# Slopes of the recurrent layer: one store per chunk from the history, in place of four stores in each step

## The chip, the cores and the metric

The program runs on one core of a Trainium2 chip, in one launch. The metric is device time in microseconds, the median of three runs. Engines are named as in the profile: PE (matmul), PEld (its weight load), DVE, ACT, POOL, and SP, whose only work here is to issue DMAs and to wait for them. SPq in a row is SP's queue of instructions.

## What is computed

A tower of five layers on 64 sequences of 248 tokens with 64 features: a convolution over tokens, attention, a sparse feed-forward layer, a recurrent layer whose weights are learned while it reads, and a mixture of experts. The change is in the fourth. Cut to what matters:

```python
def step(carry, xs):
    cp, cm = carry                       # weights W0 [64,256], W1 [256,64] and P0, P1; their momenta
    k_t, v_t, q_t, a_t, th_t, e_t = xs
    g = jax.vmap(jax.grad(loss_fn))(cp, k_t, v_t)         # mean((mlp(k) - v)^2)
    nm = m * e_t - th_t * g              # for each of the four
    np_ = p * (1 - a_t) + nm
    return (np_, nm), _mlp(np_, q_t)     # silu(h @ (W0+P0)) @ (W1+P1)
_, ys = jax.lax.scan(step, (cur_p, cur_m), xs)            # 248 steps, one after the other
```

## The kernel before

The recurrent layer (`recurrent_layer`) takes 249 steps in 16 chunks (`NCH`), `CH` = 16 steps in each of the first 15 and 9 in the last. Within a chunk the weights are not updated step by step. Each step's hidden row `h`, output row `y` and slope `dl` (the gradient at the hidden layer, 256 wide, two copies of 64 sequences) go to a history on chip, `hist`, whose partition is 16 times a group of sequences plus the step, and later steps read the past from there. At the head of the next chunk, the update, the 16 steps are folded into the weights.

The first layer's weights are handled differently: a step needs only the product of keys and weights, so the update works it out for the 16 coming steps ("base") from all earlier slopes. These lie in memory, in `DXD` (the profile calls it between_slopes), one row of 64 x 256 numbers for each step. The update reads them back in pieces of 512 KB into a ring of three tiles that share space with `hdiag` (`load_slopes`, L2091), 16 pieces in chunks 0 to 8 and 32 in chunks 9 to 15. A table of products of keys, `CT`, comes in beside them (`load_table`, L2085).

SP works its instructions off in the order in which they are written:

- at a chunk's head: wait until the other engines have begun the chunk; four or six loads of the table; wait for `hist_d`, the semaphore on which all of the last chunk's slopes count; three loads of slopes; then eight loads `cc` (L2137) and eight `alt` (L2142); then, as PE finishes each of 16 groups ("bg"), more loads of slopes and tables and the stores of the base (L2156);
- in each step: load the base of the next step (L2063), eight copies of `h` to the history (`to_hist`, L2074), load a value (L2066), eight copies of `y` and one store of it (L2176), eight copies of `dl` to the history, and four stores of `dl` to `DXD` (L2180). The copies and the stores of `dl` count on one semaphore, `hist_d`: 8 + 4 DMAs in each step.

The lines that wait for slopes on PE: in a step, before the first matmul that reads the history of slopes (L2330), for the twelve DMAs of the step before; in the update, before the matmuls of each group X (L2287), for the pieces in the ring. The update on PE is a chain over X = 0 to 15: `new_terms` (L2254), `turned` (L2267), `from_slopes` (L2280 with the table's first part, L2287 with the slopes). PE goes on to the next X only when it is through with `from_slopes` of this one.

Of the kernel before, what the change touches and what calls it, by code (L numbers as in the profile page):

```python
# [11 lines left out]
B, L, D, DIN, HID = 64, 248, 64, 128, 256  # L12
TL = L // 2
FS = 8
NH = 8
CH, NCH = 16, 16
# [24 lines left out]
class Space:  # L41
# [8 lines left out]
    def sem(self, name):  # L50
        return self.ctx.enter_context(self.nc.semaphore(f"{self.name}_{name}"))
# [48 lines left out]
def settled(e, sem):  # L100


    e.nop().then_inc(sem, 1)
# [884 lines left out]
def key_layer(nc, W_fused, H2, ZR, VR, GR, DXD, CT):  # L988
# [3 lines left out]
    with ExitStack() as ctx:  # L992
# [3 lines left out]
        zero = S.sb("zero", [128, 64 * D])  # L996
# [6 lines left out]
        s_own, s_own_sp, s_own_pe = S.sem("settled"), S.sem("settled_sp"), S.sem("settled_pe")  # L1003
        s_id, s_w, s_z, s_v, s_t = S.sem("ident"), S.sem("weights"), S.sem("zeros"), S.sem("set_v"), S.sem("set_t")
# [7 lines left out]
        out = Loop(S.sem("out"), ["z"], 16 * 8, 0)  # L1012
        with nc.Block() as block:
# [10 lines left out]
            @block.sync  # L1024
            def _(e):
                e.dma_start(wr[:, 0, :], W_fused[0:128, :]).then_inc(s_w, 16)
                e.dma_start(wr[0:NF - 128, 1, :], W_fused[128:NF, :]).then_inc(s_w, 16)

                e.wait_ge(s_v, 1)
                z3 = lambda k: zero[:, 0:k * D].rearrange("p (t d) -> p t d", d=D)  # L1030
                nz = 0
                for t0 in range(0, VR.shape[0], 64):
                    k = min(64, VR.shape[0] - t0)
                    e.dma_start(VR[t0:t0 + k, :, :].rearrange("t p d -> p t d"), z3(k)).then_inc(s_z, 16)
                    nz += 1
                e.dma_start(ZR[0:CH + 1, :, :].rearrange("t p d -> p t d"), z3(CH + 1)).then_inc(s_z, 16)
                k = ZR.shape[0] - CH - L
                e.dma_start(ZR[CH + L:, :, :].rearrange("t p d -> p t d"), z3(k)).then_inc(s_z, 16)
                e.dma_start(GR[L:, :, :].rearrange("t b g -> t (b g)"), zero[0:CH * NCH - L, 0:4 * B]).then_inc(s_z, 16)
                nz += 3  # L1040
                for t0 in range(0, CH * NCH, 32):
                    e.dma_start(DXD[t0:t0 + 32, :, :].rearrange("t b f -> (t b f)").rearrange("(p f) -> p f", p=128), zero[:, :]).then_inc(s_z, 16)
                    nz += 1
                for c0, c1, r0, r1 in ((0, 4, 128, 192), (9, 12, 256, 320)):
                    for c in range(c0, c1):
                        e.dma_start(CT[c, r0:r1, :, :], zero[0:64, 0:2048].rearrange("p (g f) -> p g f", g=16)).then_inc(s_z, 16)
                        nz += 1

                e.wait_ge(s_z, 16 * nz)
                with e.Fori(0, 4) as j:  # L1050
                    with e.Fori(0, 4) as q:
                        n = 4 * j + q
                        VE.wait(e, n, "kn")
                        settled(e, s_own_sp)
                        AE.wait(e, n, "v")
                        settled(e, s_own_sp)
                        for a in range(2):
                            t0 = TL * a
                            for w, (dst, row) in enumerate(((ZR[CH + 1 + t0:CH + 1 + t0 + TL], 16), (ZR[CH + t0:CH + t0 + TL], 0), (VR[t0:t0 + TL], 0))):
                                e.dma_start(dst[:, bass.ds(32 * j + 4 * q + row, 4), :], kqv[:, w, a:8:2, :]).then_inc(out.sem, 16)  # L1060
                            e.dma_start(GR[t0:t0 + TL, bass.ds(4 * n, 4), :], gt[:, a:8:2, :]).then_inc(out.sem, 16)
                out.count(e, B // 4)
# [546 lines left out]
RT = 64 + CH * NCH  # L1609
# [222 lines left out]
def recurrent_layer(nc, CT, DXD, VR, GR, YR, BASED, W0, P0, W1, P1):  # L1832
# [8 lines left out]
    with ExitStack() as ctx:  # L1841
# [3 lines left out]
        def sem(name):  # L1845
            return ctx.enter_context(nc.semaphore(name))

        HD, D = 256, 64
# [5 lines left out]
        hist = sb("hist", [128, 8, 2 * HD + D])  # L1854
# [18 lines left out]
        dl = sb("dl", [128, HD])  # L1873
# [17 lines left out]
        DX = 3  # L1891

        ring = [hdiag[:, :, :, :, :].rearrange("p a r j f -> p (a r j f)")[:, 1024 * q:1024 * q + 1024].rearrange("p (j f) -> p j f", j=4) for q in range(DX)]
# [4 lines left out]
        b = [t[:, :] for t in bank]  # L1898
# [45 lines left out]
        base_out = [Stages(sem(f"base_out{q}"), [f"b{k}" for k in range(q, 8, 2)], [], 2 * 16) for q in range(2)]  # L1944
# [4 lines left out]
        value_in = Stages(sem("value_in"), ["first"], ["next"], 16)  # L1949
        hist_h = Stages(sem("hist_h"), [], ["h"], 16 * NH)  # L1950
        hist_y = Stages(sem("hist_y"), [], ["y"], 16 * (NH + 1))
        hist_d = Stages(sem("hist_d"), [], ["d"], 16 * (NH + 4))
        for q in (*sum(dx_in, []), *sum(ct_in, []), *base_out, gates_in, cc_in, al_in, base_in, value_in, hist_h, hist_y, hist_d):
            q.base = 0
        s_set, s_own = sem("set_dma"), sem("settled")
        s_own_pe = sem("settled_pe")
# [119 lines left out]
        def load_gates(e, c):  # L2076
            for q in range(8):
                e.dma_start(gates[16 * q:16 * q + 16, :, :],
                            GR[bass.ds(c * CH, CH), 16 * (q // 2):16 * (q // 2) + 16, :].rearrange("t b g -> b t g")).then_inc(gates_in.sem, 16)

        def load_table(e, c, part, y):

            nb = PARTS[part][2]
            for k, (r0, r1) in enumerate(((0, 64), (64, 192), (192, 320))[:nb + 1]):
                e.dma_start(ct[0:r1 - r0, y % 2, k, :, :].unsqueeze(1), CT[bass.ds(c, 1), r0:r1, 2 * y:2 * y + 2, :].rearrange("a r g f -> r a g f")).then_inc(ct_in[part][y % 2].sem, 16)  # L2085

        def load_slopes(e, part, xk):

            nb = PARTS[part][2]
            g, k = divmod(xk, nb)  # L2090
            e.dma_start(ring[xk % DX], DXD[128 * k:128 * k + 128, g:B:16, :]).then_inc(dx_in[part][xk % DX].sem, 16)  # L2091

        def diag_h(hf):
            return ap(hdiag, hf * 2048, [16, 8], [129, 16])
# [10 lines left out]
        with nc.Block() as block:  # L2105
# [14 lines left out]
            def _(e):  # L2120
                def chunk(c, steps, part):
# [6 lines left out]
                    for yk in range(2):  # L2128
                        load_table(e, c, part, yk)
                    e.wait_ge(hist_d.sem, c * (hist_d.unit * CH))  # L2130
                    settled(e, s_own)
                    for xk in range(DX):
                        load_slopes(e, part, xk)
# [29 lines left out]
                    for s in range(steps):  # L2163
                        e.wait_ge(V.sem, V.step(c, s - 1, "xb") if s else V.upd(c, "x0"))
                        load_base(e, s + 1)

                        e.wait_ge(V.sem, V.step(c, s, "h"))
                        to_hist(e, s, h[:, :], 0, HD, hist_h.sem)
                        if s == 0 and steps == CH:
                            load_gates(e, c + 1)  # L2170
                        e.wait_ge(V.sem, V.step(c, s, "y1"))
                        settled(e, s_own)
                        load_value(e, c, s + 1)
                        e.wait_ge(V.sem, V.step(c, s, "y"))
                        to_hist(e, s, y[:, 0, :], HD, HD + D, hist_y.sem)
                        e.dma_start(YR[bass.ds(c * CH + s, 1), :, :].rearrange("a p d -> p a d"), y[:, 0:1, :]).then_inc(hist_y.sem, 16)  # L2176
                        e.wait_ge(V.sem, V.step(c, s, "d"))
                        to_hist(e, s, dl[:, :], HD + D, 2 * HD + D, hist_d.sem)
                        for j in range(4):
                            e.dma_start(DXD[bass.ds(c * CH + s, 1), 16 * j:16 * j + 16, :].rearrange("a p d -> p a d"),  # L2180
                                        dl[32 * j:32 * j + 16, :].unsqueeze(1)).then_inc(hist_d.sem, 16)

                for part, (first, last, nb) in enumerate(PARTS):
                    with e.Fori(first, min(last, NCH - 1)) as c:
# [356 lines left out]
def audio_tower(nc, x, filt, W_k, b_k, Wqk, Wv, Wpos, bpos, Wproj, bproj, gating, wr, br, w1, b1, w2, b2,  # L2541
                W_fused, W0, W1, P0, P1, Wg, bg, E1, be1, E2, be2, out):

    def scratch(name, *shape):
        return nc.dram_tensor(f"between_{name}", shape, F32, kind="Internal").ap()


    H0, X0, H1, H2, XN = (scratch(n, B, TL, 2, D) for n in ("h_tok", "x_att", "h_att", "h_ffn", "x_ffn"))
    T_ = CH * NCH
    ZR, VR, YR = scratch("keys", T_ + CH + 1, 128, D), scratch("values", T_ + 1, 128, D), scratch("recurrent", T_, 128, D)  # L2550
    GR = scratch("gates", T_, B, 4)
    DXD, CT = scratch("slopes", T_, B, HID), scratch("table", NCH, RT, 16, 128)
    token_layer(nc, x, filt, W_k, b_k, H0, X0)
    attention_layer(nc, Wqk, Wv, Wpos, bpos, Wproj, bproj, gating, H0, X0, H1)
    ffn_layer(nc, wr, br, w1, b1, w2, b2, H1, H2, XN, scratch("w_by_tile", B, L), scratch("w_by_batch", B, L))
    key_layer(nc, W_fused, H2, ZR, VR, GR, DXD, CT)
    table_layer(nc, ZR, GR, CT)
    recurrent_layer(nc, CT, DXD, VR, GR, YR, scratch("base", CH + 1, 128, HID), W0, P0, W1, P1)
    expert_layer(nc, Wg, bg, E1, be1, E2, be2, H2, YR, out)
# [29 lines left out]
```

## Time and profile before

| | |
|---|---|
| median of three runs | 12295.05 us (12288.87 to 12295.21) |
| the profiled execution | 12288.19 us, its span 12286.5 us |
| PE / DVE / ACT busy | 79% / 38% / 16% of the span |
| recurrent layer | from about 3255 us to 11082 us of the span |
| a step | 24.2 us, 249 of them |
| an update | 78 us (chunk 0), 87 to 106 us (chunks 1 to 8), 118 to 135 us (chunks 9 to 15) |
| granted clock of PE | 0.99 in the steps, 0.54 to 0.81 in the updates |

Read it from the outside in: the recurrent layer is nearly two thirds of the span; inside it, steps and updates alternate; each has its own chain of waits.

### The profile page before, as it was taken

How to read it: one execution, taken by the hardware profiler on the slowest of the kernel's cores; microseconds unless marked ns; L12 is line 12 of the kernel's file. 1: busy time of each engine (PE TensorE's matmuls, PEld its weight loads, DVE VectorE, ACT ScalarE, POOL GpSimd, SP SyncE). 2: the span in 40 equal slices, each digit the busy share in tenths (PEclk: the TensorE clock that was granted, in tenths of full speed). 3: DMA queues.
4: the chain of work that ended last, by engine and by line, in shares of the span. 5: the costliest groups of instructions: out<-in, count | busy, mean ns of one | idle time of the engine just before them, and what ended most of it. 6: DMA issues, size and time to landing. Idle time of an engine off the chain costs nothing. (4 is left out here: it accounts for less than half of the span.)

```text
span 12286.5 us, 338221 instructions
## 1 busy us (share of the span) xinstructions
PE 9695.2 (79%) x135922; PEld 5708.6 (46%) x135922; DVE 4669.4 (38%) x11974; ACT 1960.7 (16%) x4398; POOL 232.7 (2%) x167
## 2 busy tenths in 40 slices
PE   5788883523598888888988988889888898896777
PEld 2455551212355555555555555555455555552222
DVE  3444443634723323233233233232332323235555
ACT  1222221211101101011011011110101101012334
POOL 0000000000100000000000000000000000000000
PEclk7999996555898998999999999989898798987888
DMA  2000000143601101011011011120211202020000
GB/s 55 7 7 8 7 8 25 42 123 61 138 17 53 51 18 52 23 47 53 17 53 53 17 53 57 42 81 17 82 45 54 81 17 82 26 72 14 13 10 10
DMA packets 894399, 519.70 MB, mean 42 GB/s; under 512 B 379950, under 2 KB 889462, under 8 KB 892534
## 3 DMA queue, kind: packets, MB, share of 16 engines
q1 hardware_dynamic: 880694, 502.37, 15.1%
q0 software_dynamic: 13312, 12.57, 0.6%
q8 instruction: 188, 3.08, 0.1%
q14 instruction: 205, 1.68, 0.0%
HBM read 323.24 MB, written 154.20 MB: 39 GB/s over the span
## 5 line engine op out<-in xcount | busy, mean ns | idle before, releaser
L2319 PE MATMUL bank<-mv,hdiag 128*32 128x144 f32 x63744 | 2038.0, 289 | 102.1 <-DVE hdiag L2480 102.1
L2319 PEld LDWEIGHTS bank<-mv,hdiag 128*32 128x32 f32 x63744 | 1950.0, 111 | 165.8 <-DVE hdiag L2480 151.2
L2359 PE MATMUL bank<-mvt,ydiag 128*32 128x512 f32 x15936 | 1830.3, 594 | 0.0
L2359 PEld LDWEIGHTS bank<-mvt,ydiag 128*32 128x32 f32 x15936 | 606.5, 109 | 807.8 <-issue 723.1
L2493 DVE TENSOR_TENSOR rep<-bank,wt 128x128 f32<-128x128 f32 x249 | 92.0, 369 | 1863.1 <-PE bank L2319 1863.1
L439 PE MATMUL att_bank<-att_ka,att_qn 128*124 128x496 f32 x1024 | 497.0, 598 | 133.6 <-DVE att_mx L616 67.0
L2423 DVE SCALAR_TENSOR_TENSOR mvt<-mvt,cu,bank 128x256 f32<-128x256 f32 x512 | 223.3, 478 | 791.3 <-PE bank L2254 791.3
L2216 ACT ACTIVATE work<-work 128x128 f32<-128x128 f32 x498 | 142.3, 309 | 2357.6 <-DVE work L2468 2357.6
L2203 ACT ACTIVATE mv<-bank 128x256 f32<-128x256 f32 x1024 | 325.1, 384 | 1091.1 <-PE bank L2267 1091.1
L459 PE MATMUL att_bank<-att_qa,att_ka 128*124 128x248 f32 x2048 | 464.7, 385 | 32.6 <-DVE att_qa L625 32.6
L2254 PE MATMUL bank<-hist,wy 32*128 32x256 f32 x2048 | 393.1, 544 | 90.4 <-DVE wy L2413 89.7
L1555 DVE TENSOR_TENSOR moe_hw<-moe_hb,moe_bank 128x496 f32<-128x496 f32 x512 | 326.4, 669 | 354.5 <-ACT moe_hb L1414 287.0
L2224 ACT ACTIVATE mv<-hdiag 128x128 f32 x249 | 107.8, 433 | 2047.7 <-PE bank L2319 2047.7
L2522 DVE TENSOR_SCALAR work<-bank,wt 128x256 f32<-128x256 f32 x249 | 120.6, 484 | 824.1 <-PE bank L2359 824.1
L2267 PE MATMUL bank<-r_ident,mvt 128*128 128x128 f32 x2048 | 403.9, 362 | 34.6 <-DVE mvt L2431 33.9
L1336 PE MATMUL moe_bank<-moe_x,moe_w 128*128 128x496 bf16 x1536 | 416.8, 415 | 0.0
L459 PEld LDWEIGHTS att_bank<-att_qa,att_ka 128*124 128x124 f32 x2048 | 345.9, 186 | 144.4 <-DVE att_qa L625 48.8
L2287 PE MATMUL bank<-hdiag,ct 128*32 128x256 f32 x2944 | 313.4, 531 | 124.0 <-DMA hdiag<-between_slopes 123.9
L616 DVE TENSOR_REDUCE att_mx<-att_bank 124x2 f32<-124x496 f32 x512 | 339.1, 673 | 166.9 <-PE att_bank L439 163.2
L2267 PEld LDWEIGHTS bank<-r_ident,mvt 128*128 128x128 f32 x2048 | 320.4, 186 | 165.7 <-issue 97.9
L2519 DVE TENSOR_TENSOR ddiag<-bank,mi 128x128 f32<-128x128 f32 x249 | 72.7, 292 | 848.8 <-PE bank L2357 848.8
L2372 PE MATMUL bank<-mvt,r_ident 128*128 128x256 f32 x1494 | 389.0, 396 | 0.0
(402 smaller groups left out, 11450.9 us busy)
## 6 DMA issues: line engine op xcount, KB each, us to landing
hdiag<-between_slopes SPq DMA_DIRECT2D x368, 512.0 KB, 4.6
baset<-between_base SPq DMA_DIRECT2D x265, 128.0 KB, 2.0
between_base<-work SPq DMA_DIRECT2D x256, 128.0 KB
hist<-h SPq DMA_DIRECT2D x1992, 8.0 KB
hist<-y SPq DMA_DIRECT2D x1992, 2.0 KB
hist<-dl SPq DMA_DIRECT2D x1992, 8.0 KB
ct<-between_table SPq DMA_DIRECT2D x184, 128.0 KB, 3.8
between_slopes<-key_zero SPq DMA_DIRECT2D x8, 2048.0 KB
```

What stands on the lines that cost most here:

```text
L439: e.matmul(bank[3 + i % 2][0:TL, 0:2 * L], qn[:, TL * a:TL * a + TL], ka[:, 2 * hp:2 * hp + 2, :], start=True, stop=True).then_inc(T.sem, 1)
L459: mm = e.matmul(bank[3 + h % 2][0:TL, L * mh:L * mh + L], ka[:, h, TL * mh:TL * mh + TL], qa[:, :], start=True, stop=True)
L616: e.tensor_reduce(mx[:, i // 4, 2 * (i % 4):2 * (i % 4) + 2], bank[3 + i % 2][0:TL, 0:2 * L].rearrange("p (h m) -> p h m", h=2), AX, ALU.m ...
L1336: mm = e.matmul(bank[2 + 2 * a + q][:, 0:2 * L], w[:, x_, 128 * a:128 * a + 128], xp[:, 2 * L * q:2 * L * q + 2 * L], start=(k == 0), stop ...
L1555: e.tensor_tensor(hw[:, a, q, :], hb[:, a, q, :], bank[q][:, 0:2 * L], ALU.mult).then_inc(V.sem, 1)
L2203: e.activation(dst, src, ACT.Copy).then_inc(A.sem, 1)
L2254: mm = e.matmul(psNew[X % 2][k][:, HD * w:HD * w + HD], wy[rows, G % 2, w, :, :].rearrange("p u d -> p (u d)"), hist[rows, m * 4 + j, 0:HD ...
L2267: mm = e.transpose(psC[k][:, o:o + 128], mvt[:, 4 * n + j, HD * w + 128 * hf:HD * w + 128 * hf + 128], ident[:, :])
L2287: mm = e.matmul(out[rows, :], ct[:, yk % 2, 1 + k, g % 2, rows], ring[xk % DX][:, j, :], start=False, stop=(k == nb - 1))
L2319: mm = e.matmul(psP[32 * j:32 * j + 32, 0:MW], hdiag[:, hf, r, j, :], mv1[:, hf, r, j, :], start=(hf == 0 and r == 0), stop=(hf == 1 and r ...
L2359: mm = e.matmul(psH[32 * j:32 * j + 32, :], ydiag[:, n, j, :], mvt[:, 4 * n + j, :], start=(n == 0), stop=(n == 7))
L2372: e.matmul(b[1][:, HD:], ident[:, :], mvt[:, k, 0:HD], start=True, stop=True)
```

## The change

The four stores in each step go. At a chunk's head, after the wait for `hist_d`, SP stores the slopes of the last chunk from the history, eight stores of 128 KB (8 groups of 8 sequences, 16 steps each), waits until all eight have landed on a new semaphore `slopes_out`, and loads the first pieces then. `hist_d` counts eight DMAs in each step. `DXD` gets 16 rows in front, so that chunk c can write rows 16c to 16c + 15; chunk 0 writes the zeros with which the history starts. The slopes of the last chunk are not stored, and nobody reads them.

```diff
-        hist_d = Stages(sem("hist_d"), [], ["d"], 16 * (NH + 4))
+        hist_d = Stages(sem("hist_d"), [], ["d"], 16 * NH)
+        slopes_out = Stages(sem("slopes_out"), ["out"], [], 8 * 16)
...
+        SLOPES = DXD[0:CH * NCH, :, :]
...
-            e.dma_start(ring[xk % DX], DXD[128 * k:128 * k + 128, g:B:16, :]).then_inc(dx_in[part][xk % DX].sem, 16)
+            e.dma_start(ring[xk % DX], DXD[CH + 128 * k:CH + 128 * k + 128, g:B:16, :]).then_inc(dx_in[part][xk % DX].sem, 16)
...
                     e.wait_ge(hist_d.sem, c * (hist_d.unit * CH))
+                    settled(e, s_own)
+                    for m in range(2):
+                        for j in range(4):
+                            dst = SLOPES[bass.ds(c * CH, CH), 16 * j + 8 * m:16 * j + 8 * m + 8, :].rearrange("t b f -> b t f")
+                            e.dma_start(dst, hist[:, m * 4 + j, HD + D:]).then_inc(slopes_out.sem, 16)
+                    e.wait_ge(slopes_out.sem, slopes_out.upd(c, "out"))
                     settled(e, s_own)
                     for xk in range(DX):
                         load_slopes(e, part, xk)
...
                         to_hist(e, s, dl[:, :], HD + D, 2 * HD + D, hist_d.sem)
-                        for j in range(4):
-                            e.dma_start(DXD[bass.ds(c * CH + s, 1), 16 * j:16 * j + 16, :].rearrange("a p d -> p a d"),
-                                        dl[32 * j:32 * j + 16, :].unsqueeze(1)).then_inc(hist_d.sem, 16)
...
-    DXD, CT = scratch("slopes", T_, B, HID), scratch("table", NCH, RT, 16, 128)
+    DXD, CT = scratch("slopes", T_ + CH, B, HID), scratch("table", NCH, RT, 16, 128)
```

SP's queue at the head of a chunk before the change, from the last two loads of the table on (ct) to the first of cc; hdiag<-between_slopes are the loads of slopes:

```order
L2085 DMA ct<-between_table 64x256
L2085 ISA
L2085 DMA ct<-between_table 128x256
L2130 REGISTER_ALU
L2091 DMA hdiag<-between_slopes 128x4x256 [waits hist_d]
L2091 DMA hdiag<-between_slopes 128x4x256 x2
L2137 ISA
L2137 DMA cc<-between_table 16x2x128
```

The same place after it; between_slopes<-hist are the new stores, of which the first three and the last stand here:

```order
L2088 DMA ct<-between_table 128x256
L2133 REGISTER_ALU
L2138 ISA [waits hist_d]
L2138 DMA between_slopes<-hist 8x16x256
L2138 ISA
L2138 DMA between_slopes<-hist 8x16x256
...
L2138 ISA
L2138 DMA between_slopes<-hist 8x16x256
L2139 ISA
L2094 DMA hdiag<-between_slopes 128x4x256 [waits slopes_out]
L2094 DMA hdiag<-between_slopes 128x4x256 x2
L2146 ISA
```

Eight stores and a wait for their landing have moved in ahead of the first load of slopes, and with it ahead of all that SP does later in the update.

SP's queue at the end of the first step of a chunk, before the change:

```order
L2074 DMA hist<-y 8x64 x7
L2176 DMA between_recurrent<-y 128x64
L2177 REGISTER_ALU
L2074 DMA hist<-dl 8x256 [waits vector_landed]
L2074 DMA hist<-dl 8x256 x7
L2180 ISA
L2180 DMA between_slopes<-dl 16x256
L2180 ISA
L2180 DMA between_slopes<-dl 16x256
```

And after it:

```order
L2075 DMA hist<-y 8x64 x7
L2185 DMA between_recurrent<-y 128x64
L2186 REGISTER_ALU
L2075 DMA hist<-dl 8x256 [waits vector_landed]
```

Behind the eight copies of `dl` the four stores, each with an instruction ahead that works out its address, are gone, and the next step's load of the base stands there; SP works nothing else off in a different order.

## Rows read from the trace of the kernel before

**Rows 1.** The page: the whole span.

```profile
span 12286.5 us, 338221 instructions
```

**Rows 2.** Waits of SP's queue in the recurrent layer: us in total, times, longest.

```profile
SPq L2074 <- DVE work L2468: 1143.8, 189, 6.5
...
SPq L103 <- DMA between_base<-work: 34.2, 16, 2.2
...
SPq L2189 <- DMA between_slopes<-dl: 1.1, 1, 1.1
```

**Rows 3.** Waits of PE over the whole span, the two for DMAs in the updates.

```profile
PE bank L2287 <- DMA hdiag<-between_slopes: 123.9, 56, 5.1
...
PE bank L2280 <- DMA ct<-between_table: 63.5, 15, 5.0
```

**Rows 4.** Waits of PE in 4820 to 5195 us (15 steps), all of them.

```profile
PE bank L2310 <- DVE h L2475: 16.2, 15, 1.1
PE bank L2323 <- DVE rep L2493: 9.3, 16, 0.6
PE bank L2319 <- DVE hdiag L2480: 6.2, 15, 0.4
PE bank L2345 <- DVE y L2506: 3.3, 16, 0.2
```

**Rows 5.** Timeline of one step: start, length, instructions [idle before].

```profile
5007.94 4.87 SPq L2074 DMA_DIRECT2D hist<-dl  x8
...
5013.01 1.87 SPq L2180 DMA_DIRECT2D between_slopes<-dl  x4
...
5019.32 0.64 PE L2330 MATMUL bank<-hist,adiag 128*32 128x256 f32 x8
5019.43 0.29 DVE L2499 TENSOR_TENSOR gdiag<-bank,mi 128x128 f32<-128x128 f32 x1 [0.39 <-PE bank L2323]
...
5019.89 0.27 PEld L2340 LDWEIGHTS bank<-hist,gdiag 128*32 128x32 f32 x16 [0.42 <-issue]
```

**Rows 6.** Timeline at the head of chunk 3.

```profile
4704.13 4.87 SPq L2074 DMA_DIRECT2D hist<-dl  x8
...
4709.20 1.86 SPq L2180 DMA_DIRECT2D between_slopes<-dl  x4
...
4714.34 3.04 SPq L2085 DMA_DIRECT2D ct<-between_table  x4
4717.59 1.96 SPq L2091 DMA_DIRECT2D hdiag<-between_slopes  x3
4717.82 1.08 PE L2280 MATMUL bank<-w,ct 64*32 64x256 f32 x8 [4.97 <-DMA ct<-between_table]
4719.84 5.93 SPq L2137 DMA_DIRECT2D cc<-between_table  x8
4722.42 1.08 PE L2287 MATMUL bank<-hdiag,ct 128*32 128x256 f32 x8 [3.52 <-DMA hdiag<-between_slopes]
```

**Rows 7.** SP's stores of the base, 128 KB each: issue in ns min/median/max.

```profile
L2156 SPq DMA_DIRECT2D between_base<-work x256: 572/607/701, 3286.2 to 10844.3; - x128
```

**Rows 8.** DMA issues by tile: count, KB each, median us from issue to landing.

```profile
between_table<-tab_ci SPq DMA_DIRECT2D x16, 512.0 KB, 5.6
...
cc<-between_table SPq DMA_DIRECT2D x128, 16.0 KB, 3.0
```

**Rows 9.** Windows: 16 steps, then whole updates (chunks 3, 5, 11, 13); length, busy, PEclk, DMA share, GB/s.

```profile
4812.00:5200.00 388.00, 352.03 (x7158) 226.77 (x7162) 108.44 (x362) 30.74 (x96) 0.00 (x0) 0.99 0.07 17
...
4705.00:4811.00 106.00, 84.58 (x518) 45.17 (x518) 45.70 (x119) 25.43 (x72) 4.19 (x2) 0.60 0.40 120
...
5688.00:5775.00 87.00, 64.31 (x518) 35.29 (x518) 45.34 (x117) 24.58 (x72) 4.19 (x2) 0.76 0.48 147
...
8638.00:8765.00 127.00, 93.98 (x646) 48.60 (x646) 45.23 (x119) 25.33 (x72) 4.19 (x2) 0.64 0.56 175
...
9678.00:9813.00 135.00, 108.41 (x646) 56.45 (x646) 46.04 (x121) 25.76 (x72) 4.19 (x2) 0.54 0.53 165
```

**Rows 10.** Timeline at the head of chunk 0.

```profile
3269.94 1.96 SPq L2091 DMA_DIRECT2D hdiag<-between_slopes  x3
...
3276.88 1.08 PE L2287 MATMUL bank<-hdiag,ct 128*32 128x256 f32 x8
```

**Rows 11.** Timeline at the end of the layer.

```profile
11074.38 4.83 SPq L2074 DMA_DIRECT2D hist<-dl  x8
11079.25 1.82 SPq L2180 DMA_DIRECT2D between_slopes<-dl  x4
11082.67 0.29 SPq L1251 DMA_DIRECT2D moe_wgr<-in_L_ffn_Wg_dram  x1
```

More of the change, by code:

```diff
@@ L1041, in _ @@
                 for t0 in range(0, CH * NCH, 32):
-                    e.dma_start(DXD[t0:t0 + 32, :, :].rearrange("t b f -> (t b f)").rearrange("(p f) -> p f", p=128), zero[:, :]).then_inc(s_z, 16)
+                    e.dma_start(DXD[CH + t0:CH + t0 + 32, :, :].rearrange("t b f -> (t b f)").rearrange("(p f) -> p f", p=128), zero[:, :]).then_inc(s_z, 16)
                     nz += 1
@@ L1951, in recurrent_layer @@
         hist_y = Stages(sem("hist_y"), [], ["y"], 16 * (NH + 1))
-        hist_d = Stages(sem("hist_d"), [], ["d"], 16 * (NH + 4))
-        for q in (*sum(dx_in, []), *sum(ct_in, []), *base_out, gates_in, cc_in, al_in, base_in, value_in, hist_h, hist_y, hist_d):
+        hist_d = Stages(sem("hist_d"), [], ["d"], 16 * NH)
+        slopes_out = Stages(sem("slopes_out"), ["out"], [], 8 * 16)
+        for q in (*sum(dx_in, []), *sum(ct_in, []), *base_out, gates_in, cc_in, al_in, base_in, value_in, hist_h, hist_y, hist_d, slopes_out):
             q.base = 0
```

## The prediction

> **What bounds the kernel now.** I read the waits of PE first, because PE is busy for most of the recurrent layer, and then the waits of SP, because the change touches SP's queue alone. Nothing else is edited: matmuls, vector work, and the number and size of loads stay. So the question is only which of SP's times anybody waits for.
>
> In the steps nobody waits for it. In a window of 15 steps all waits of PE end with DVE, none with a DMA [rows 4], while SP itself waits for DVE, 1143.8 us in 189 waits under one line alone [rows 2]: SP is the one that is early. The transfer that could be late is the step's last, since PE must have the twelve DMAs of the step before by its first matmul on the history of slopes. In the timeline of a step the copies of dl are issued from 5007.94 us and the stores from 5013.01 to 5014.88 us; after the layer's very last store SP waited 1.1 us until all had landed [rows 2], so these had by about 5016.0. PE comes to them at 5019.32 us [rows 5]: 3.3 us to spare, and by then it has just ended the matmul ahead of it.
>
> In the updates the opposite holds. At the head of chunk 3 SP issues the table at 4714.34 us, and PE, which has been ready since 4712.86, waits 4.97 us for it; SP issues the slopes at 4717.59, and PE waits 3.52 us for them, to 4722.42 [rows 6]. Over the span there are 63.5 us in 15 waits for the table and 123.9 us in 56 for slopes [rows 3]. Here the path runs through SP: ends of copies of dl, four stores, a branch, the table's loads, the first load of slopes, its landing, PE. What SP is given to do before 4717.59 moves PE, one for one, and with PE the rest of the update, since every later X stands behind the first, and SP's later loads stand behind the stores too.
>
> **What the change removes.** In steps 0 to 14 of a chunk the four stores are hidden, as above: removing them gives nothing. That is 4 x 0.5 us of queue time a step, and SP only waits longer for DVE. In a chunk's last step they lie on the path that leads to the next head: the copies end at 4709.00, the stores at 4711.06 [rows 6], so all behind them comes 2.06 us earlier. The gain for the table's load is worth nothing by itself, because PE then waits that much longer for the slopes.
>
> A rule of the Trainium skill speaks for the change beyond that: the page "DMA: Bandwidth & Descriptors", section Bandwidth, says to batch transfers, and that those under 64 KB are bound by their descriptors. Sixty-four stores of 16 KB become eight of 128 KB. In the rows the small ones take 1.87 us for four, so 30 us of queue time a chunk against some 6; but this time is not on the path, and by the rows the saving is 2.06 us a chunk. Were it all on the path, that rule would take 16 x 24 = 380 us off, less the landings; that case is the first rival below.
>
> **What it adds, at each head.** First, the issue of eight stores. The trace has the same transfer under another name: the stores of the base are 128 KB from 128 partitions, issued in 0.607 us [rows 7]. Theirs have fixed addresses; the new ones get an address from a register in the loops. Four stores of that kind take 1.87 us at about 0.32 us of issue each, so 0.19 us lies between two [rows 5]. I take 0.61 + 0.19 = 0.80 us, eight times: 6.3 us. Second, the landing of the last. After the last stores of the base SP waited 34.2 / 16 = 2.14 us [rows 2]; I take that, as size, direction and place in the queue are alike. Third, one more wait with its settling instruction, 0.1 us. Together 8.5 us; less the 2.06, the first load of slopes is issued 6.5 us later.
>
> The bounds: at the least, issue as fast as the small stores (0.5 us apart, 4.0 us) and landing like the layer's last one (1.1 us), 5.2 us with the settling, net 3.1 us. At the most, the transfer itself is the limit: stores of 512 KB to memory land in 5.6 us [rows 8], so 1 MB in 11.2 us, net 9.2 us. I stay with 6.5, since the stores of the base are the nearest row in every respect. It is no matter that SP's next loads, those of cc with 5.93 us of issue and more behind them, come after it: they stood behind the slopes before too [rows 6], and the whole queue moves.
>
> Nothing hides it, since PE's wait for the slopes was still 3.52 us long before. Fifteen chunks give 15 x 6.5 = 97 us. Chunk 0 is different: there the slopes were issued at 3269.94, and PE came to them at 3276.88 without a wait [rows 10]. No stores fall away, so the issue comes at 3278.5; from issue to matmul it was 4.83 us in chunk 3, which gives 3283.3 us, 6.4 us later. At the layer's end four stores less stand before the next layer, whose first load is at 11082.67 and would start 1.9 us earlier [rows 11].
>
> **The sum.** 97 + 6.4 - 1.9 = 102 us on 12288.2 us of the profiled execution (span 12286.5, [rows 1]), 12390 us. The median of the runs shown is 12295.05, the lowest 12288.87, so the profiled execution stands at their lower end; I put the median at 12393, 0.8% slower than before. By the bounds the additions are 15 x 3.1 + 3 - 2 = 48 us and 15 x 9.2 + 9 - 2 = 145 us: 12336 and 12440 us.
>
> **The clock's share.** PE is granted 0.99 in the steps and 0.54 to 0.76 in the updates [rows 9]: its clock falls to 1.2 GHz in the idle time at a head and comes back to 2.4 GHz some tens of microseconds into the work. The same work took 87 us in chunk 5 at 0.76 and 106 us in chunk 3 at 0.60, and 127 against 135 us at 0.64 and 0.54 in the larger updates [rows 9]. The head was idle before and is idle for longer now, so the fall is there already; I assume that the return comes as long after the restart as before, and add nothing. But the draw in each of 16 updates is new. Single updates differ by up to 19 us, mostly by less than 7; some sixteen independent draws of that size would shift the sum by about 25 us either way.
>
> **The rivals.**
> - SP's queue is the bound of the steps, and 1.87 us less of it shortens them: up to 249 x 1.87 = 466 us less, against 16 x 8.5 = 136 us more at the heads, 11958 us; with as little as 0.41 us a step (102 / 249) it evens out. This ends on the other side. It would need SP to be late in a step; the wait rows say that SP waits for DVE and PE never for SP [rows 2, 4]. Chance 2%.
> - PE's unnamed 0.42 us ahead of L2340 in every step [rows 5] is a wait for the history's DMAs, and goes: 249 x 0.42 = 105 us less, which cancels the loss, 12290 us. Against it: DVE's gdiag ends at 5019.72, and the weights are loaded at 5019.89, just behind it. Chance 3%.
> - The clock comes back at a time counted from its fall, not from the restart: then each update does 6.5 us more of its work at the high level. What that is worth comes from [rows 9]: the time at the low level is 2 x (1 - granted clock) x length, 85 us in chunk 3 and 42 in chunk 5, 43 us less for an update 19 us shorter, 0.44 us for each; for the larger updates 124 and 91 us, 33 us less for 8 us, 0.24 for each. So 9 x 2.9 + 7 x 1.6 = 37 us come back: 12356 us. Chance 12%.
> - The longer idle time makes the return later or less stable, so that updates look more like chunks 3 and 13 than like 5 and 11. Half the way to those for half the chunks is 8 x 9.5 = 76 us or less for the small ones and a few for the large: I price it at 50 us, 12443 us. Chance 13%.
> - The stores are slower than those of the base, because eight in a row fill the queues: 9.2 us net, 12440 us, as above. Chance 8%.
>
> **How the numbers follow.** The forecast has the remaining 62%, with its own range 12365 to 12420 from the issue (0.7 to 0.9 us each) and the clock's draw. Leaving out the two cheap rivals and half of each tail, the range that should hold 8 in 10 is 12345 to 12445 us. A measurement of this kernel tells 0.2%, some 25 us, from no change: faster 3%, same 4%, slower 93%.
>
> **What would show it.** In the changed kernel, at a head: eight stores of about 0.6 us issue in 6.3 us; a wait of SP's queue for them of 2.1 us in 16 cases, 34 us in all; the table's matmul two microseconds earlier, and PE's wait for slopes there 3.5 + 8.6 = 12.1 us long, some 250 us in all in place of 123.9 (with chunk 0's own). Steps of 24.2 us as before. Updates 6.5 us longer on average, at about the same granted clock in the part after the restart. The prediction is wrong if steps get shorter (then SP or a transfer did bound them), if the wait after the stores is far from 2 us, or if updates grow by another amount than the heads do, which would be the clock.

## The result, and the profile after

| | before | after |
|---|---|---|
| median | 12291.96 us (4 runs, 12281.11 to 12295.21) | 12397.42 us (4 runs, 12362.7 to 12406.76) |
| ratio, 95% interval | | 1.0082 (1.0062 to 1.0103) |
| profiled span | 12286.5 us | 12396.3 us |
| sum over 16 updates, scan to first matmul on slopes ("head") | 263.4 us | 375.4 us |
| sum over 16 updates, from there to the first step ("rest") | 1454.8 us | 1441.8 us |
| sum over 16 chunks, the steps | 6065.4 us | 6075.0 us |

The changed kernel is slower by 0.8%, forecast 12393 us. The last three lines are worked out from the starts in the traces: of DVE's scan `ut` at a chunk's head, of the first matmul on slopes (L2287 before, L2293 after), of the first step's first DVE instruction, and of the last `dl`. They share out the 109.8 us between the two profiled spans: heads +112.0, rest of the updates -13.0, steps +9.6, layers ahead of this one +5.1, end of this layer and all behind it -3.9.

The timeline at the head of chunk 3 in the changed kernel, which answers to [rows 6] (start, length, what, count, [idle before]):

```profile
4716.19 4.87 SPq L2075 DMA_DIRECT2D hist<-dl  x8
...
4717.43 0.80 DVE L2403 TENSOR_TENSOR_SCAN ut<-te,td 128x306 f32<-128x306 f32 x1
...
4724.44 2.97 SPq L2088 DMA_DIRECT2D ct<-between_table  x4
...
4727.77 6.62 SPq L2138 DMA_DIRECT2D between_slopes<-hist  x8
...
4727.91 1.08 PE L2286 MATMUL bank<-w,ct 64*32 64x256 f32 x8 [3.00 <-DMA ct<-between_table]
4736.78 1.97 SPq L2094 DMA_DIRECT2D hdiag<-between_slopes  x3
4739.03 5.98 SPq L2146 DMA_DIRECT2D cc<-between_table  x8
...
4741.19 1.08 PE L2293 MATMUL bank<-hdiag,ct 128*32 128x256 f32 x8 [12.20 <-DMA hdiag<-between_slopes]
```

From the copies of dl to the table it is now 8.25 us in place of 10.21, so the four stores have gone from the path. What is left of it is 4.87 us of copies and, for the most part, the branch at the end of SP's loop over chunks: it is issued at 4721.19 us, and the next instruction stands at 4723.93 us. Eight stores take 6.62 us, and their landing another 2.4 until the loads of slopes go out. PE waits 12.20 us for slopes instead of 3.52.

Waits of SP's queue in the recurrent layer, and of PE over the span, answering to [rows 2, 3]:

```profile
SPq L103 <- DMA between_slopes<-hist: 37.9, 16, 3.0
SPq L103 <- DMA between_base<-work: 35.6, 16, 2.2
...
SPq L2195 <- DMA hist<-dl: 1.1, 1, 1.1
```

```profile
PE bank L2293 <- DMA hdiag<-between_slopes: 245.1, 39, 12.7
...
PE bank L2286 <- DMA ct<-between_table: 37.4, 15, 4.3
```

The wait for between_slopes<-hist is the new one, 2.37 us each. The timeline at the end of the layer, which answers to [rows 11]:

```profile
11188.02 4.83 SPq L2075 DMA_DIRECT2D hist<-dl  x8
11194.50 0.32 SPq L1251 DMA_DIRECT2D moe_wgr<-in_L_ffn_Wg_dram  x1
```

From the last copies of dl to the next layer's first load it is 6.48 us in place of 8.29. Windows of 16 steps and of the updates of chunks 3, 6 and 13 (length; busy of PE, PEld, DVE, ACT, POOL; PEclk; DMA share; GB/s), answering to [rows 9]:

```profile
4808.00:5198.00 390.00, 353.93 (x7168) 233.99 (x7168) 110.09 (x367) 30.77 (x96) 0.00 (x0) 0.99 0.06 14
...
4717.00:4808.00 91.00, 58.06 (x518) 32.22 (x518) 46.57 (x122) 24.52 (x73) 4.20 (x2) 0.80 0.50 151
6165.00:6267.00 102.00, 71.18 (x518) 38.71 (x518) 45.23 (x118) 24.90 (x72) 4.19 (x2) 0.68 0.44 135
9760.00:9902.00 142.00, 108.83 (x646) 56.40 (x646) 45.38 (x118) 25.85 (x72) 4.20 (x2) 0.53 0.53 163
```

Chunk 3 has a longer head than before and yet a shorter update, 91 us against 106, because the granted clock was 0.80 and not 0.60. Whoever compares this one update sees the change win. Only sums over all sixteen, or the heads apart from the rest, can be read.

### The profile page after: what moved, and what is told of

Read it like the earlier page. It is cut to its first block and busy times, and to the rows that moved or that the text cites. A ratio compares the mean times of both kernels' runs of the same rounds, so it can differ in the third digit from the quotient of the medians.

```text
span 12396.3 us, 335440 instructions
## 1 busy us (share of the span) xinstructions
PE 9704.1 (78%) x135922; PEld 5787.7 (47%) x135922; DVE 4668.7 (38%) x11974; ACT 1959.8 (16%) x4398; POOL 233.0 (2%) x167
## 5 line engine op out<-in xcount | busy, mean ns | idle before, releaser
L2365 PEld LDWEIGHTS bank<-mvt,ydiag 128*32 128x32 f32 x15936 | 689.1, 109 | 738.5 <-issue 546.8
L2293 PE MATMUL bank<-hdiag,ct 128*32 128x256 f32 x2944 | 317.4, 544 | 245.2 <-DMA hdiag<-between_slopes 245.1
```

Of the source, the lines that this page charges most:

```text
L2293: mm = e.matmul(out[rows, :], ct[:, yk % 2, 1 + k, g % 2, rows], ring[xk % DX][:, j, :], start=False, stop=(k == nb - 1))
L2365: mm = e.matmul(psH[32 * j:32 * j + 32, :], ydiag[:, n, j, :], mvt[:, 4 * n + j, :], start=(n == 0), stop=(n == 7))
```

## The experiments

Each but the last was run in several executions beside the kernel before. All measured sums are gathered in a table behind them. The runs without stores, with the late wait and with four stores leave out all or half of the past slopes, and their loads read zeros there; the others compute everything.

**The added part alone.** The kernel before, its stores in the steps kept, and at each head the same stores to a tensor that nobody reads:

```diff
                     e.wait_ge(hist_d.sem, c * (hist_d.unit * CH))
                     settled(e, s_own)
+                    for m in range(2):
+                        for j in range(4):
+                            dst = SLOPES[bass.ds(c * CH, CH), 16 * j + 8 * m:16 * j + 8 * m + 8, :].rearrange("t b f -> b t f")
+                            e.dma_start(dst, hist[:, m * 4 + j, HD + D:]).then_inc(slopes_out.sem, 16)
+                    e.wait_ge(slopes_out.sem, slopes_out.upd(c, "out"))
+                    settled(e, s_own)
```

> The kernel before, with the four stores in each step kept, and in addition the eight stores of 128 KB from the history and the wait for their landing at each head; they go to a spare tensor that nobody reads, and the loads read what the steps stored. Theory (the head's chain of SP is the path, and the steps do not feel SP's queue): the first matmul on slopes comes 9.1 us later in each update (the 7.0 us that the changed kernel shows and the 2.06 us that it saves), 16 updates, about 140 us, so 12430 us, within about 25 us for PE's clock in the updates. Rival (the changed kernel's loss is made elsewhere, by the clock or by the new place of the rows in memory): about 12300 us. Steps 389.5 us per 16 in both.

12423.55 us, ratio 1.0112 (1.0094 to 1.0129); heads +145.7 us. The stores and the wait alone make more than the whole loss, with the rows in memory where they were; the rival is out.

**The removed part alone.** The changed kernel without the eight stores and the wait:

```diff
-                    for m in range(2):
-                        for j in range(4):
...
-                            e.dma_start(dst, hist[:, m * 4 + j, HD + D:]).then_inc(slopes_out.sem, 16)
-                    e.wait_ge(slopes_out.sem, slopes_out.upd(c, "out"))
-                    settled(e, s_own)
```

> The changed kernel without the eight stores and the wait at the head: slopes are not stored at all, so the loads read zeros and the base leaves out the past slopes. Theory: the first matmul on slopes comes 2.06 us earlier than before the change in chunks 1 to 15, 31 us, and the layer ends 1.9 us earlier: 12260 us, within about 25 us for the clock. Rival (SP's queue or the stores weigh on the steps): steps shorter by 0.1 us or more, 25 us or more off beyond that, 12230 us or less.

12270.41 us, ratio 0.9984 (0.9971 to 0.9996); heads 30.4 us shorter, 2.0 us a chunk, as said. The median fell by 12 us only, within the 25 us left to the clock. The steps did not get shorter (6079.1 us), so SP's queue weighs on none of them.

**The wait taken off the path.** The changed kernel, the stores into a spare tensor, the wait moved behind the update's last group:

```diff
-        SLOPES = DXD[0:CH * NCH, :, :]
+        SLOPES = nc.dram_tensor("between_spare", (CH * NCH, B, HID), F32, kind="Internal").ap()
...
-                    e.wait_ge(slopes_out.sem, slopes_out.upd(c, "out"))
-                    settled(e, s_own)
                     for xk in range(DX):
                         load_slopes(e, part, xk)
...
+                    e.wait_ge(slopes_out.sem, slopes_out.upd(c, "out"))
+                    settled(e, s_own)
                     load_base(e, 0)
```

> The changed kernel with its eight stores at the same place, but into a spare tensor, and the wait for their landing at the end of the update, ahead of the first load of the base; the loads read zeros, the base leaves out the past slopes. Theory: only the landing (37.9 us over 16 updates in the changed kernel's trace) and a settling instruction go, 2.5 us a chunk, 40 us: 12357 us, within 25 for the clock; the issue of 6.5 us stays on the path. Rival (most of the 7 us is the wait for memory, the issue would be hidden): the first matmul on slopes back at 17 us after the head's scan, 12290 us.

12392.48 us, ratio 1.0086 (1.0068 to 1.0103). Its heads are 29.6 us shorter than the changed kernel's, 1.85 us each, not 2.5. The head of chunk 3:

```profile
4720.91 6.62 SPq L2138 DMA_DIRECT2D between_spare<-hist  x8
...
4727.59 1.93 SPq L2094 DMA_DIRECT2D hdiag<-between_slopes  x3
...
4732.34 1.08 PE L2293 MATMUL bank<-hdiag,ct 128*32 128x256 f32 x8 [10.11 <-DMA hdiag<-between_slopes]
```

From the loads' issue to the matmul it is 4.75 us here, against 4.41 us in the changed kernel, whose stores have landed by then; over chunks 1 to 15 the means are 4.99 and 4.35 us. So part of the wait comes back as slower loads. The issue of 6.6 us is the larger part, which the theory had right. The time, though, hardly fell (12357 us was expected); see below the table.

**The order turned round.** The changed kernel, full computation, the stores ahead of the table's loads:

```diff
-                    for yk in range(2):
-                        load_table(e, c, part, yk)
                     e.wait_ge(hist_d.sem, c * (hist_d.unit * CH))
                     settled(e, s_own)
...
+                    for yk in range(2):
+                        load_table(e, c, part, yk)
                     e.wait_ge(slopes_out.sem, slopes_out.upd(c, "out"))
```

> The changed kernel, full computation, with the eight stores issued ahead of the four or six loads of the table, so that the loads' issue (3.2 us, 3.8 in the larger updates) lies beside the landing of the stores. Theory (the order on SP's queue decides, and landing can be covered): the wait for the landing goes, 2.4 us a chunk, and the first matmul on slopes comes that much earlier, about 37 us in the sum: 12355 us, within 25 for the clock. Rival (landing is not what delays, since in the run with the late wait the first matmul moved by 1.9 us a chunk and not by 2.5): the table's loads slow the stores, and less than 1 us a chunk is won, 12385 us.

12400.84 us, ratio 1.0083 (1.0059 to 1.0107). SP's wait for the landing is gone (0.2 us in all), and the heads are 29.2 us shorter. PE now waits for the table, and then for the slopes:

```profile
4749.11 7.11 SPq L2136 DMA_DIRECT2D between_slopes<-hist  x8
...
4756.41 2.59 SPq L2088 DMA_DIRECT2D ct<-between_table  x4
...
4759.21 1.96 SPq L2094 DMA_DIRECT2D hdiag<-between_slopes  x3
...
4759.70 1.08 PE L2286 MATMUL bank<-w,ct 64*32 64x256 f32 x8 [10.14 <-DMA ct<-between_table]
...
4764.36 1.08 PE L2293 MATMUL bank<-hdiag,ct 128*32 128x256 f32 x8 [3.58 <-DMA hdiag<-between_slopes]
```

The stall moved in the direction of the theory, 1.8 us a chunk of the 2.4. The time did not follow (12355 us was expected): the rest of the updates took 1498.6 us in this profile, with 1110 us of it at 1.2 GHz, against 1441.8 and 960.

**Something else taken off the same path.** The kernel before with `dl`'s copies of a chunk's last step moved behind the fourth group of the update; the four stores now stand ahead of the copies in each step and count on a semaphore of their own, for which the loads of slopes wait, and the waits on `hist_d` are one step higher.

```diff
-                        to_hist(e, s, dl[:, :], HD + D, 2 * HD + D, hist_d.sem)
...
+                        if s < CH - 1:
+                            to_hist(e, s, dl[:, :], HD + D, 2 * HD + D, hist_d.sem)
...
+                        if g == 3:
+                            to_hist(e, CH - 1, dl[:, :], HD + D, 2 * HD + D, hist_d.sem)
```

> The kernel before, whose stores in each step count on a semaphore of their own, with the eight copies of the last step's dl (4.87 us of issue, plus 0.2) moved from ahead of the next head's loads to a place in the update behind the fourth group; the full computation. Theory (anything SP does between dl and the load of slopes is on the path, one for one): the first matmul on slopes comes 5 us earlier in 15 chunks, 76 us: 12216 us, within 25 for the clock. Rival (the copies push SP's later loads back by as much, or PE is held by something else at the head): 12270 to 12300 us.

12226.27 us, ratio 0.9953 (0.9936 to 0.9970). Heads 75.1 us shorter, as five microseconds in 15 chunks give. The median fell by 56 us; in its profile the rest of the updates was 31 us longer. It computes all of the reference and beats both kernels. The head of chunk 3:

```profile
4693.89 1.85 SPq L2182 DMA_DIRECT2D between_slopes<-dl  x4
...
4698.85 3.07 SPq L2086 DMA_DIRECT2D ct<-between_table  x4
...
4702.13 1.96 SPq L2092 DMA_DIRECT2D hdiag<-between_slopes  x3
...
4707.14 1.08 PE L2292 MATMUL bank<-hdiag,ct 128*32 128x256 f32 x8 [3.65 <-DMA hdiag<-between_slopes]
```

**The suspected cost doubled and halved, and the changed kernel again.** Sixteen stores a head, the second eight to a spare tensor; then four:

```diff
                             e.dma_start(dst, hist[:, m * 4 + j, HD + D:]).then_inc(slopes_out.sem, 16)
+                    for m in range(2):
+                        for j in range(4):
+                            dst = SPARE[bass.ds(c * CH, CH), 16 * j + 8 * m:16 * j + 8 * m + 8, :].rearrange("t b f -> b t f")
+                            e.dma_start(dst, hist[:, m * 4 + j, HD + D:]).then_inc(slopes_out.sem, 16)
```

```diff
-                    for m in range(2):
+                    for m in range(1):
```

> The changed kernel once more, for a second profile and six executions on the chip that runs the next two kernels. Theory: the sum of the waits at the heads is fixed by SP's chain, 375 us to the first matmuls on slopes as in its first profile, within 5; the rest of the updates is drawn anew by the clock, 1442 us the first time, 1420 to 1500 us. Median within 10 us of 12397. Rival (the clock's pattern belongs to a kernel): the rest comes out the same update by update.

> The changed kernel with 16 stores at each head, the eight once more to a spare tensor, and the wait for all 16. Theory (what SP issues at the head is on the path one for one): 8 x 0.83 = 6.6 us more a chunk, the first matmuls on slopes 106 us later in the sum, 12500 us, within 25 for the clock. Rival (the updates take back part of a longer head, since in the two runs whose heads were 29 us shorter in the sum the time did not fall): half of it, 12450 us or less.

> The changed kernel with only four of the eight stores at each head, so half of the sequences' slopes stay unstored and the base is computed from zeros for them. Theory: 3.3 us less a chunk, the heads 53 us shorter in the sum, 12344 us, within 25 for the clock. Rival (the updates take back part, see above): 12370 us or more.

Again: 12378.37 us, ratio 1.0084 (1.0070 to 1.0097), heads 373.2, rest 1442.7 us. Sixteen: 12493.4 us, 1.0178 (1.0163 to 1.0192), heads 472.2. Four: 12323.07 us, 1.0036 (1.0020 to 1.0051), heads 320.1. Against the repeated run, eight stores more cost 99 us in the heads and 115 in the medians, four fewer give back 53 and 55. By the medians the updates took nothing back.

**The clock.** The changed kernel with matmuls of no use in PE's idle time at the head:

```diff
+                    def warm(n):
+                        for k in range(n):
+                            e.matmul(b[4][:, HD:], ident[:, :], mvt[:, k % 4, 0:HD], start=True, stop=True)
+
+                    warm(6)
                     new_terms(0)
                     new_terms(1)
                     for X in range(16):
                         turned(X)
+                        if X == 0:
+                            warm(20)
                         from_slopes(X)
```

> The changed kernel, full computation, with matmuls whose output nobody reads in PE's idle time at the head: 6 ahead of the first new_terms, 20 ahead of the first from_slopes, about 0.5 us each at 2.4 GHz. Theory (the clock falls in the head's idle time, and its return is what differs between updates and between executions): the granted clock stays at 2.4 GHz through the head, the rest of an update after the first matmul on slopes falls from 66 to 89 us to about 62 us in chunks 1 to 8, by 5 to 15 us in the larger ones, about 150 us in all: 12250 us, and the executions scatter less. Rival (the clock falls later in the update anyway, since the update's own gaps make it fall): no more than 30 us, 12370 us.

12400.23 us, ratio 1.0078 (1.0053 to 1.0102). I had sized it too small: at 2.4 GHz the 20 matmuls, which the trace counts as 40, were through in 10.4 us, and 6.5 us of idle time stayed:

```profile
4723.70 10.44 PE L2298 MATMUL bank<-mvt,r_ident 128*128 128x256 f32 x40
4734.06 0.64 PE L2286 MATMUL bank<-w,ct 64*32 64x256 f32 x8
4741.24 1.08 PE L2293 MATMUL bank<-hdiag,ct 128*32 128x256 f32 x8 [6.54 <-DMA hdiag<-between_slopes]
```

The clock fell in that rest of the wait, as the matmul's 1.08 us for eight shows beside 0.64 just before it. So this run does not test what it was made for. The next one, the kernel with the deferred copies and 6 and 8 such matmuls, does so better, since the shorter head leaves a smaller hole:

> The kernel before with the deferred copies, full computation, and with such matmuls in the head, 6 and 8. If both effects hold and add, the sum of the deferral (about 65 us) and the clock (about 150 us): 12080 us. If the clock falls later in the update anyway: 12210 us.

12212.43 us, ratio 0.9929 (0.9906 to 0.9953). Here PE goes through the head at 2.4 GHz: 9 us of the heads are at 1.2 GHz, against 148 us with the deferred copies alone. And then the clock falls all the same, 14 to 25 us after the scan in chunks 1 to 7. Chunk 4, PE alone:

```profile
5176.28 0.64 PE L2292 MATMUL bank<-hdiag,ct 128*32 128x256 f32 x8 [0.67 <-DMA hdiag<-between_slopes]
...
5186.17 0.64 PE L2285 MATMUL bank<-w,ct 64*32 64x256 f32 x8
5190.08 1.08 PE L2292 MATMUL bank<-hdiag,ct 128*32 128x256 f32 x8 [3.27 <-DMA hdiag<-between_slopes]
```

In all seven chunks the clock fell in a wait of PE for slopes of 2.4 to 3.4 us, or within 1.1 us after its end. In chunks 3, 4 and 6 it was the wait of the fourth group, as here; in chunks 1, 2, 5 and 7 it was what was left of the wait at the head. These are times that coincide; no run took the later waits away. The rest of the updates still has 876 us at 1.2 GHz of 1456. The rival was right: the head's idle time is not the only thing that takes the clock away. Beside the kernel with the deferred copies it is 14 us less, within the intervals, although its heads are 13.5 us longer.

**Traffic or rhythm in the steps.** The changed kernel with four tiny stores in each step, which count on `hist_d` as the old ones did:

```diff
                         to_hist(e, s, dl[:, :], HD + D, 2 * HD + D, hist_d.sem)
+                        for j in range(4):
+                            e.dma_start(SPARE[bass.ds(c * CH + s, 1), 16 * j:16 * j + 1, 0:1].rearrange("a p d -> p a d"),
+                                        dl[32 * j:32 * j + 1, 0:1].unsqueeze(1)).then_inc(hist_d.sem, 16)
```

> The changed kernel with four stores of 4 bytes each in a step, to a spare tensor, where the four stores of 16 KB stood: SP's queue has its old rhythm, the traffic of 64 KB a step is still gone. Steps: 6075 to 6079 us in the sum in the three kernels without stores in the steps, 6056 to 6065 in the three with them, nearly all of it in the first half of the matmuls on the second weights, 0.12 us in most steps. If SP's rhythm does it, the sum is 6065 us or less again; if the traffic does, it stays at 6075 or more. The head is to lose its 2 us again, 30 us in the sum.

One execution, 12446.0 us; heads +25.3 us against the changed kernel, steps 6072.9 us. That is between the two sums that were expected, 6065 and 6075 us, and nearer to the second: the rhythm does not bring the shorter steps back; see the last section.

| kernel | heads, us | rest, us | of it at 1.2 GHz | steps, us | median, us |
|---|---|---|---|---|---|
| deferred copies | 188.3 | 1485.8 | 974 | 6064.1 | 12226 |
| deferred copies, matmuls of no use | 201.8 | 1455.8 | 876 | 6065.7 | 12212 |
| no stores | 233.0 | 1458.9 | 985 | 6079.1 | 12270 |
| before | 263.4 | 1454.8 | 939 | 6065.4 | 12292 (12281 to 12285 beside the experiments) |
| four stores | 320.1 | 1424.4 | 895 | 6076.7 | 12323 |
| late wait | 345.8 | 1445.9 | 944 | 6074.6 | 12392 |
| stores first | 346.2 | 1498.6 | 1110 | 6080.0 | 12401 |
| after, twice | 375.4, 373.2 | 1441.8, 1442.7 | 960, 948 | 6075.0, 6079.1 | 12397, 12378 |
| after, matmuls of no use | 380.7 | 1455.4 | 989 | 6083.8 | 12400 |
| tiny stores, one execution | 400.7 | 1466.2 | 1005 | 6072.9 | 12446 |
| added part alone | 409.1 | 1417.0 | 857 | 6055.7 | 12424 |
| sixteen stores | 472.2 | 1443.4 | 925 | 6078.6 | 12493 |

Heads come from one profile each, medians from four to eighteen executions. Medians follow the heads one for one from 188 to 472 us, within some 20 us, but for two: late wait and stores first lie 27 and 35 us above 12283 + (heads - 263). The intervals of their ratios are 22 and 29 us to either side, so neither excess is far outside them. For the second its profile shows what is in excess, time at the lower clock. For the first it does not: the profiled execution was the fastest of the six (12367 us; the others 12379 to 12400). Why these two should draw a worse clock in all executions stays open.

The scatter goes with the clock: of 18 executions of the kernel before the fastest, 12249.65 us, had a granted clock of 0.885 over its span, the slowest, 12318.13 us, 0.877.

## Why the prediction was right

**The path.** Right. The chain through SP at the head set the time and the steps did not feel SP. The removal alone, the addition alone, half and double the stores each moved the heads within some 7 us of what was expected of them.

**The stores' issue.** Predicted 0.80 us apart from the stores of the base; measured 6.62 us for eight, 0.83.

**The landing.** Predicted 2.14 us, measured 2.37 (37.9 / 16). Together the heads gained 112.0 us where the sum had 97 + 6.4 = 103.4 us. Taking the landing away gives back only 1.85 us of it, since the loads are then slower. The sum had also taken the loads as equally fast on both sides; from issue to matmul they took 4.65 us before and 4.35 us after, the mean of chunks 1 to 15. Of the two bounds, the lower is counted from 12288 us and the upper from 12295; the result lies between them from either.

**The saving at a head.** Predicted 2.06 us, measured 2.0 (30.4 us for 15 chunks).

**The end.** Predicted -1.9 us, measured -1.81: 6.48 us in place of 8.29 from the last copies of dl to the next layer's first load.

**The steps.** Predicted nothing, measured +9.6 us: a term that was missing, and small.

**The clock.** Nothing was added for it, with 25 us either way. The rest came out 13.0 us shorter, and a second profile repeated it within 1 us. But this sum hides two moves: chunks 1 to 8 took 58.8 us less, with 161 us at 1.2 GHz in place of 312, and chunks 9 to 15 took 43.1 us more, with 773 us in place of 607.

The assumption behind the missing term, that the clock returns as long after the restart as before, failed both ways. In both kernels the clock fell within 4.4 us of the scan in chunks 1 to 15. From the first matmul on slopes to its return it took 18 to 66 us in chunks 1 to 8 before the change, and 7 to 36 us after it. In chunks 9 to 15 the first return came after 8 to 21 us before, and after 93 to 106 us in the changed kernel. Why, no run here shows. The two clock rivals, a return counted from the fall and a later return, each had the direction right for one half of the chunks, but not the size: the first was to give back 26 us in the small updates. That the halves nearly cancelled was luck, and so is part of the close number: the heads took 8.6 us more than the sum had and the steps 9.6, against which stood the 13.0 us less of the rest.

I had also treated the clock as a draw that each execution makes anew. The second profile says otherwise in part: chunks 1 to 5 took 66.1 to 68.1 us in it and 66.2 to 68.0 in the first, and chunk 6 was the longest of the small ones in both, 86 and 77 us.

**The other rivals.** Faster steps are out by the run without stores; PE's unnamed 0.42 us did not go with the stores (103.4 us over 249 steps in both profiles); the stores were not bound by the transfer, since in the kernel with sixteen the second eight were issued in 5.53 us at the head of chunk 3, no slower than the first. SP spent 6.6 us a chunk on issuing what took 30 before. The Trainium skill (page "DMA: Bandwidth & Descriptors", section Bandwidth) says to batch, and that transfers under 64 KB are dominated by their descriptors; the queue's time in this trace agrees in direction. But nobody waited for those 30.

## What to carry to other kernels

Here a transfer spread over steps in which its queue had slack cost nothing; gathered up where consumers stand and wait for what comes behind it on the same queue, each microsecond of its issue counted, and most of its landing on top. Before batching, ask in which stage somebody waits for the queue; and then look what else can leave that stage: the copies that were moved off it gave 0.5%. Where the clock moves single stages by 20 us, compare sums of waits, not one stage, and time many executions.

## What the hardware showed beyond that

In the steps, the group of 64 matmuls on the second layer's weights takes longer when the 16 KB stores are gone. The page's rows of that group for the kernel before, the added part alone, the deferred copies (all with such stores), then for the changed kernel and the one with tiny stores:

```profile
L2359 PE MATMUL bank<-mvt,ydiag 128*32 128x512 f32 x15936 | 1830.3, 594 | 0.0
```

```profile
L2367 PE MATMUL bank<-mvt,ydiag 128*32 128x512 f32 x15936 | 1825.7, 594 | 0.0
```

```profile
L2364 PE MATMUL bank<-mvt,ydiag 128*32 128x512 f32 x15936 | 1827.4, 594 | 0.0
```

```profile
L2365 PE MATMUL bank<-mvt,ydiag 128*32 128x512 f32 x15936 | 1845.2, 594 | 0.0
```

```profile
L2369 PE MATMUL bank<-mvt,ydiag 128*32 128x512 f32 x15936 | 1842.8, 594 | 0.0
```

All four profiles with stores of 16 KB in the steps (1825.7 to 1830.3 us) lie below all nine without them (1842.8 to 1849.2 us). In the starts of the matmuls it is an offset that appears with the group's fourth matmul, in the median step 1.05 us after the start of DVE's ydiag in place of 0.93, and stays. The starts of the first 32 matmuls span 3.06 us in 156 of 249 steps before the change; in the changed kernel they do so in 18, and in 152 of the steps they span 3.18 to 3.20 us. Stores of 4 bytes in the same places don't remove it, so it is not SP's rhythm; what the traffic does to PE, no run here shows.
